# Grouping TensorE's instructions by how they divide the array, in a four-layer graph network

## The reference

```python
# L0, gated edges
z = concat([x[dst], x[src], edge_attr])
m = sigmoid(z @ W_f + b_f) * softplus(z @ W_s + b_s) * exp(-distance ** 2 / 18)
out = segment_sum(m, dst) + x
# L1, plain edges
m = relu(concat([h[src], h[dst], e]) @ W1 + b1) @ W2 + b2
# L2, two attention layers with 5 heads, self loops added to the edges
xl, xr = x @ Wl + bl, x @ Wr + br
alpha = einsum(leaky_relu(xl[src] + xr[dst]), att)
out = segment_sum(softmax_over_dst(alpha) * xl[src], dst).mean(heads) + bias
# after both: h @ Wfc + bfc
# L3: degree-scaled sum over edges, linear, batch norm over the nodes, elu, added to its input
```

## Time and profile before

| | us |
|---|---|
| median of three runs | 5698.8 (5698.16 to 5701.34) |
| profiled execution | 5692.45 |
| its span, first to last instruction | 5690.7 |
| TensorE busy | 4263.5 (75%) |
| VectorE busy | 3250.9 (57%) |
| ScalarE busy | 3088.8 (54%) |
| GpSimd busy | 3317.9 (58%) |

### The profile page before, as it was taken

One profiled execution on the slowest core, in us unless ns is written; L12 is line 12 of the kernel. 1 busy time (PEld: TensorE's weight loads), 2 busy tenths in 40 slices (PEclk: granted clock), 3 DMA queues, 4 the chain that ended last, 5 costly groups with the idle time before them and its releaser, 6 DMA issues. The chain is left out here.

```text
span 5690.7 us, 126079 instructions
## 1 busy us (share of the span) xinstructions
PE 4263.5 (75%) x32065; PEld 3093.0 (54%) x32065; DVE 3250.9 (57%) x7165; ACT 3088.8 (54%) x7416; POOL 3317.9 (58%) x3341
## 2 busy tenths in 40 slices
PE   1089996599952999974997679999299896055573
PEld 1067775477741666643773256666177663055552
DVE  3934446688876332237879832233688788722266
ACT  0279996565655444433872234444178423755547
POOL 0966662377733555535878965554188687677720
PEclk6599997799976999986999989999699898577775
DMA  9476664766657445441334454444133333722224
GB/s 250 91 153 149 149 149 84 157 130 128 128 114 194 116 115 116 115 94 31 84 75 94 95 127 115 115 114 115 37 75 83 78 88 79 153 52 52 53 58 142
DMA packets 1392328, 618.39 MB, mean 109 GB/s; under 512 B 876801, under 2 KB 1351357, under 8 KB 1390426
## 3 DMA queue, kind: packets, MB, share of 16 engines
q1 hardware_dynamic: 1307692, 534.90, 39.9%
q0 software_dynamic: 63360, 65.01, 6.9%
q10 hardware_dynamic: 21140, 17.02, 1.1%
HBM read 379.93 MB, written 236.09 MB: 108 GB/s over the span
## 5 line engine op out<-in xcount | busy, mean ns | idle before, releaser
L920 ACT ACTIVATE hot_e<-iota_n,rel 128x256 f32<-128x256 f32 x1176 | 500.9, 500 | 424.2 <-PE part_e L933 418.2
L1964 DVE COPY zT_l<-zTp_l 128x512 f32<-128x512 f32 x196 | 135.6, 692 | 955.3 <-PE alp_l L1882 691.2
L1939 ACT ACTIVATE leak_l<-tp_l,bcat 128x512 f32<-128x512 f32 x588 | 391.8, 686 | 469.6 <-PE tp_l L1894 445.5
L950 DVE TENSOR_TENSOR acc<-acc,part_e 128x128 f32 x1176 | 336.3, 286 | 472.0 <-PE part_e L933 342.6
L933 PE MATMUL part_e<-z_e,hot_e 128*128 128x128 f32 x1568 | 282.5, 354 | 383.8 <-DVE acc L1661 187.0
L1036 POOL DMA_INDIRECT z_l<-g_d,src_i x392 | 384.0, 979 | 316.4 <-PE zTp_l L1075 220.8
L1036 POOL DMA_INDIRECT z_l<-h_d,src_i x392 | 383.8, 979 | 316.6 <-PE zTp_l L1075 220.9
L1036 POOL DMA_INDIRECT z_e<-h_d,src_i x392 | 384.6, 981 | 207.9 <-PE zTp_e L1075 112.9
L1944 ACT ACTIVATE leak_l<-tp_l,bcat 128x256 f32<-128x256 f32 x784 | 307.1, 474 | 350.2 <-PE tp_l L1901 348.4
L933 PEld LDWEIGHTS part_e<-z_e,hot_e 128*128 128x128 f32 x1568 | 260.2, 259 | 406.1 <-DVE acc L1661 187.3
L1170 POOL DMA_INDIRECT z_e<-h_d,row_of_e x392 | 387.2, 988 | 124.6 <-issue 108.8
(11 more groups left out here) (408 smaller groups left out, 11426.3 us busy)
## 6 DMA issues: line engine op xcount, KB each, us to landing
m_d<-m_m SPq DMA_DIRECT2D x196, 138.0 KB
h_d<-h SPq DMA_DIRECT2D x56, 448.0 KB
relb_e<-rel_d SPq DMA_DIRECT2D x196, 128.0 KB
near_e<-h_d SPq DMA_DIRECT2D x392, 64.0 KB
near_e<-g_d SPq DMA_DIRECT2D x392, 64.0 KB
relb_l<-rel_d SPq DMA_DIRECT2D x196, 128.0 KB
near_l<-h_d SPq DMA_DIRECT2D x392, 64.0 KB
z_l<-rest_d SPq DMA_DIRECT2D x196, 128.0 KB
```

Of the source, the lines that this page charges most:

```text
L920: ins = self.nc.scalar.activation(self.hots[k][:, t, :], self.S["iota_n"][:, :], ACT.Abs, scale=-1.0, bias=self.S["rel"][:, ds(n * BLK + t ...
L950: ins = self.nc.vector.tensor_tensor(x, x, part[:, t % 2, :, 0:x.shape[2]], ALU.add)
L1939: nc.scalar.activation(leak[u % 2][:, q, :], tp[q][:, :], ACT.Relu, bias=bcat[:, 0, q:q + 1], scale=1.0 - SLOPE).then_inc(leak_ready, 1)
```

## The change

`turn` gets two parameters. With a step of 4, the logits and e0 now do all four transposes of a block first and then the eight one-hot products of all four tiles (sixteen instructions). In e0 the two attribute transposes, with their waits, stand between the two. The e0 bias and the a1 bias become products over all 128 rows of the array in bf16: three rows carry the parts of the bias, the others are zero. For that the bias of a1 is cut into three bf16 parts in `setup`, as the one of e0 was already, and two tiles are cleared there. In `node_tables` the ring of `sq` has three buffers instead of four, and the wait that guards it moves by one group.

```diff
-        bias3 = sb("bias3", [3, BLK * C], BF16)
-        ones3 = sb("ones3", [3, P], BF16)
+        bias3 = sb("bias3", [P, BLK * C], BF16)
+        bfc3 = sb("bfc3", [P, BLK * C], BF16)
+        ones3 = sb("ones3", [P, P], BF16)
...
+                chain(nc.vector.memset(S["bias3"][:, :], 0.0))
+                chain(nc.vector.memset(S["bfc3"][:, :], 0.0))
...
+                for i in range(3):
+                    chain(nc.vector.tensor_copy(cut_b[:, 0:C], S["bfc"][0:3, :]))
+                    chain(nc.vector.tensor_copy(cut[:, i, 0:C], cut_b[:, 0:C]))
+                    chain(nc.vector.tensor_tensor(S["bfc"][0:3, :], S["bfc"][0:3, :], cut[:, i, 0:C], ALU.subtract))
+                chain(nc.vector.tensor_scalar(whole[:, 0:C], cut[:, 0, 0:C], ident[0:3, 0:1], None, ALU.mult))
+                for i in range(1, 3):
+                    chain(nc.vector.scalar_tensor_tensor(out=whole[:, 0:C], in0=cut[:, i, 0:C], scalar=ident[0:3, i:i + 1], in1=whole[:, 0:C],
+                                                         op0=ALU.mult, op1=ALU.add))
+                chain(nc.vector.tensor_copy(S["bfc3"][0:3, :].rearrange("p (q c) -> p q c", q=BLK), wide(whole[:, 0:C], 1, BLK)))
...
-        xc, sq, h = (sb(n, [P, GRP, C]) for n in ("xc", "sq", "h"))
+        xc, sq, h = (sb(n, [P, GRP, C], deep) for n, deep in (("xc", DEEP), ("sq", DEEP - 1), ("h", DEEP)))
...
-                    need(act, n_var, g - DEEP + 1)
-                    nc.scalar.activation(sq[g % DEEP][:, :, :], xc[g % DEEP][:, :, :], ACT.Square).then_inc(n_sq, 1)
+                    need(act, n_var, g - DEEP + 2)
+                    nc.scalar.activation(sq[g % (DEEP - 1)][:, :, :], xc[g % DEEP][:, :, :], ACT.Square).then_inc(n_sq, 1)
...
-    def turn(self, pe, n, u, i, zTp, gathered):
+    def turn(self, pe, n, u, i, zTp, gathered, step=2, between=None):
...
-        for r in range(0, BLK, 2):
-            for t in (r, r + 1):
+        for r in range(0, BLK, step):
+            for t in range(r, r + step):
                 self.nc.tensor.matmul(zTp[:, t * P:(t + 1) * P], self.z[k][:, t, :], ident[:, :], start=(t == 0), stop=False, is_transpose=True, skip_group_check=True)
+            if between is not None:
+                between()
             for w in range(WIN):
-                for t in (r, r + 1):
+                for t in range(r, r + step):
...
-                    near.turn(pe, n, u, i, zTp, gathered)
-                    pe.wait_ge(att_in[k], 32 * (i + u // RINGS + 1))
-                    need(pe, aT_ready, n)
-                    for q in range(2):
-                        tr = nc.tensor.transpose(aTp[:, q * P:(q + 1) * P], att[k][:, 2 * q:2 * q + 2, :].rearrange("p t c -> p (t c)"), ident[:, :])
-                    tr.then_inc(att_used, 1)
+                    def turn_att():
+                        pe.wait_ge(att_in[k], 32 * (i + u // RINGS + 1))
+                        need(pe, aT_ready, n)
+                        for q in range(2):
+                            tr = nc.tensor.transpose(aTp[:, q * P:(q + 1) * P], att[k][:, 2 * q:2 * q + 2, :].rearrange("p t c -> p (t c)"), ident[:, :])
+                        tr.then_inc(att_used, 1)
+                    near.turn(pe, n, u, i, zTp, gathered, BLK, turn_att)
...
-                    near.turn(pe, n, u, i, zTp[u % 2], gathered)
+                    near.turn(pe, n, u, i, zTp[u % 2], gathered, BLK)
...
-                    nc.tensor.matmul(fcp[:, :, :], S["ones"][0:1, 0:P], wide(S["bfc"][0:1, :], 1, BLK), start=True, stop=False,
+                    nc.tensor.matmul(fcp[:, :, :].rearrange("p t c -> p (t c)"), S["ones3"][:, :], S["bfc3"][:, :], start=True, stop=False,
                                      skip_group_check=True)
```

More of the change, by code:

```diff
@@ L508, in _ @@
                                                          op0=ALU.mult, op1=ALU.add))
-                chain(nc.vector.tensor_copy(S["bias3"][:, :].rearrange("p (q c) -> p q c", q=2), wide(whole[:, :], 1, 2)))
+                chain(nc.vector.tensor_copy(S["bias3"][0:3, :].rearrange("p (q c) -> p q c", q=2), wide(whole[:, :], 1, 2)))
+                for i in range(3):
[7 more added lines that the diff above has]
+                chain(nc.vector.tensor_copy(S["bfc3"][0:3, :].rearrange("p (q c) -> p q c", q=BLK), wide(whole[:, 0:C], 1, BLK)))
                 chain(nc.vector.tensor_reduce(bl_one[:, :], bl_col[:, :], AX.X, ALU.add))
@@ L788, in spread @@
                     need(dve, n_std, g - DEEP + 1)
-                    nc.vector.tensor_reduce(var[g % DEEP][:, :], sq[g % DEEP][:, :, :], AX.X, ALU.add).then_inc(n_var, 1)
+                    nc.vector.tensor_reduce(var[g % DEEP][:, :], sq[g % (DEEP - 1)][:, :, :], AX.X, ALU.add).then_inc(n_var, 1)
                 def normalise(g):
```

## The result

The changed kernel takes 5611.1 us (5609.95 to 5611.1) against 5700.1 for the one before on the same chip: ratio 0.9847, interval 0.9833 to 0.986. The forecast was 5610 and faster. The medians differ by 89 us, as forecast; the spans of the two profiled executions differ by 82.6 (5690.7 and 5608.1), and by stage the terms of the sum did not all come out.

| stage, us | before | after | difference | forecast |
|---|---|---|---|---|
| setup | 141.4 | 142.7 | +1.3 | +3.8 |
| gated edges e0 | 638.0 | 620.3 | -17.7 | -26 |
| l0 and l1 | 821.8 + 821.3 | 794.2 + 794.5 | -54.4 | -58 |
| a1 | 305.8 | 292.9 | -12.9 | -9 |
| node_tables | 189.0 | 188.8 | -0.2 | 0 |

The account below looks back on a forecast made before the run. TensorE, busy all the time in e0, l0 and a1, was taken as the bound. Logits -58, e0 -26, a1 -9 and setup +4 sum to -89 us: 5610 from the median 5698.8, range 5592 to 5634.

Parts of the forecast that it names:

- Logits: l0 and l1: turn 1.91 to 1.61 us, period 7.20 to 6.90, 58 us saved (bounds 53 to 60).
- ScalarE's wait for the half-row projections: Logits: ScalarE waits 1.80 us a block for the projections; predicted to go down to 1.5 after the change.
- the 1.80 us of waiting: Logits: ScalarE's wait per block for the projections, cited against its stores of logits taking part of the gain.
- rival 4: Logits: ScalarE's stores between its relus push these into the projections, half of .30 is lost: 5639 us; chance 0.08.
- e0: Gated edges: period 6.14 to 5.87 us, set by ScalarE and TensorE together, 26 us saved (bounds 16 to 33).
- end of the hot tiles, .12 to the scatter: Gated edges: first term of the 5.79 us chain, .12 us from ScalarE's hot tiles to TensorE's scatter.
- rival 2: Biases of e0 and a1: full-height bf16 product still pays a change each side; e0 gains 12, a1 0: 5633; chance 0.05.
- a1: Second pass over the nodes: .10 us a block saved over 90 blocks, 9 us (bounds nothing and 38).
- two-block loop: Second node pass: turn_back waits for GpSimd's total, resting on a projection two blocks before; .20 free in two periods.
- Setup: Kernel opening: thirteen chained VectorE instructions cost 3.3 us and two memsets .5 us, +3.8 us.
- Node tables: node_tables: ring of three instead of four waits for nothing new, 0 us; outer estimate 70 us in all.
- Sum: Whole kernel: -58 - 26 - 9 + 4 = -89 us, giving 5610 against the median of 5698.8.

Follow-up runs that it names:

- l_turn: The kernel before with the step of 4 in the logits alone, on a chip where the kernel before takes 6039 us: ratio 0.9949 (0.9932 to 0.9965).

## Why the prediction was right, term by term

**Logits: right.** Turn 1.61 and period 6.90, each as said, to .01. The transposes of a pass lie 28.9 us closer together (694.2 to 665.3); the stages shrank by 27.6 and 26.8, since 1 to 2 us came back behind the last block, where the statistics of the softmax run. I didn't trace these. The measured 54.4 lie within the bounds of 53 to 60. Two things of this part were wrong and cost nothing here: ScalarE's wait for the half-row projections did not fall to 1.5, and the 1.80 us of waiting held against rival 4 said nothing of the relus that stand behind the stores. What rules it out on this chip is that TensorE never waits for them.

**e0: mechanism right, size off.** The mis-sized term is the chain's "end of the hot tiles, .12 to the scatter". It had no row. The trace shows .24 to .30, mostly .25, in the changed kernel; in the later ones of this chip's pace the shortest is .23 or .24, and in the kernel before the scatter never started sooner than .25 either. With it the chain is 5.92, and (5.92 + 5.95)/2 = 5.94, against 5.96 measured and 5.87 said. That explains .07 of the .09; .02 stay open. The .09 on 95 blocks are the 8 us by which e0 fell short (17.7 for 26); the value lay in the bounds of 16 to 33. Of the other terms of the chain those that can be read stood: bias at .11 an instruction with no change beside it (rival 2 out), transposes at .11, .32 to the copy. What the prediction did not ask is which of TensorE's instructions lie inside the loop. It counted the turn with the attribute transposes in it, rightly, but never saw that they needn't be there.

**a1: right, size low.** The two-block loop was named and shows itself as an alternation of 2.6 and 3.1; 2.86 measured for 2.87 said. The stage lost 12.9 and not 9, since .12 a block came free and not .10, over 98 blocks and not 90, and about 1 us at the stage's ends. I had allowed .16 of the .36 between total and transpose for load and signal; the trace after shows .06. So more of it was slack.

**Setup: the instructions right (3.25 for 3.3), the sum not shown.** Its sign is hidden by weights that arrive at 119.5 to 125.1 us from run to run.

**Node tables: right.** 188.8 us against 189.0.

**Sum.** The terms give -83, the forecast was -89, and the medians show -89. The difference is in the profiled run of before, which lies 7.6 us under its median, while the one of after lies 1.1 under its own. The 1 us between forecast and median is therefore partly luck: e0 fell short by 8 and the logits by 4, a1 gave 4 more, and setup cost 2.5 less. The kernel before alone spreads over 13 us from run to run on a later chip (5689.0 to 5702.3). Nor do the stated bounds give the 5594 to 5631 of the forecast: added end to end they give 5571 (5601 with a1 at its forecast) and 5634.

## What to carry to other kernels

Where two engines wait for each other in turn, the period is the length of that loop over the blocks it spans, and only what lies inside it counts: in e0 the same TensorE instructions gave 11 us more when two of them were moved out of the loop, and work moved off the other engine gave half of its length. Where blocks alternate between two lengths, as in e0 and a1 here, look for such a loop. In a1 it was relieved by letting it span one more block without changing the order inside a block; a change of the order made a worse loop (72 us) at a shared buffer. Before you take a time from a measured period and a difference, add up the loop's own terms and the engines' own periods as well: the next limit may be closer than the difference says. And an idle stretch that a profile puts down to one engine can be filled with DMA issues, which it doesn't count as busy.

## What the runs showed of the hardware that I had not expected

- From the end of ScalarE's instruction to TensorE's first instruction that waits for it: .24 to .30 us in the blocks of e0, where GpSimd's total to TensorE's transposes in a1 shows .06 (ends on GpSimd are rough).
- A full-height bf16 product of 256 columns between fp32 ones takes .11 us to the next instruction, and its start is .11 after the neighbour ahead (e0 of the changed kernel). With 3 rows it took .12 to the second one, .21 from the neighbour ahead and .20 to the one behind (e0 of the kernel before).
- Chips differ: the kernel before took 5695 to 5700 us in three of the four comparisons and 6039 in the one on a chip where e0 waits for loads (in `l_turn` 71 of 240 us on VectorE, at a granted clock of .98) and the logits for a store. There the bias of e0, worth 13.7 us in that stage elsewhere, gave nothing that can be told from no change (1.0004).
